# Group norm folded into per-image weights, context and attention products on quarter-width column tiles

## Chip, cores and metric

One Trainium2 chip, one of its cores. The metric is the device time of one launch in microseconds; the median of three runs of the kernel before is 2759.55 us (2758.84 to 2760.31).

## What is computed

The input x is float32 of shape (4, 128, 112, 112). Two residual blocks follow each other, each behind a group norm (32 groups of 4 channels):

```python
x = x + _L0_conv_ref(_gn(x), ...)   # layer norm over channels, 8x8 window attention, 8 heads of 16
x = x + _L1_conv_ref(_gn(x), ...)   # linear attention, depthwise 3x3, projection, batch norms, MLP
```

The second block, with t the 12544 tokens of an image:

```python
q, k, v = relu(t @ Wq + bq) * scale, relu(t @ Wk + bk), t @ Wv + bv
ctx = einsum('bhnd,bhne->bhde', k, v)      # 16x16 for each head, summed over all tokens of the image
out = einsum('bhnd,bhde->bhne', q, ctx)    # then depthwise 3x3, Wproj, batch norm 1 with t
ff = gelu(t @ Wfc1 + bfc1) @ Wfc2 + bfc2   # 128 -> 1024 -> 128, batch norm 2
```

## The kernel before, in words

Channels lie on the 128 partitions, and one whole image of float32 lies in `ximg` (128 x 12544). The work has three stages, each of which runs over the four images.

**Stage A**, window attention: `group_loop` (each engine has its own copy, with a `step` written out by hand) runs over strips of 8 rows (14 for an image, 56 in all), and in each strip over two groups, of 4 and of 3 pairs of windows (`gg` 0 and 1). A group is computed over several steps. In the step of group G, TensorE runs in this order (lines 1348 to 1381): `score_rows` of G (line 1289, coarse scores for the maxima), `out_transpose` of G-2 (1328), half 1 of `attend` of G-1 (1320, probabilities times values), `ln_transpose` of G+2 (1244), `out_project` of G-2 (1334), half 0 of `attend`, `transpose_maxima` (1295), the query and key projections of G+1 (1255 to 1257), `score_cols` (1304, 1309), `project_v` of G+1 (1272) and `ln_back` of G+2 (1250). VectorE runs `maxima` (940), `normalise` of half 1 (953, 957), `ln_stats` (911), `mt_evac` (946), `ln_moments` (919), `normalise` of half 0, in odd groups the statistics of x1 (963), `ln_norm` (926), `v_evac` of G+1 (933) and, in images 0 to 2, statistics of the next image (963) at even groups. ScalarE evacuates and does the exponentials (663); GpSimd the low halves, casts, reciprocal roots (508) and the residual (542). The query projection waits until half 1 is normalised, since they share bank 7 (line 1371).

In `attend` each 64x64 block of probabilities is the stationary operand and goes to partitions 64*w2 of the output; so two column tiles of 64 are in use, with 128 rows.

**Stage C**, keys, values and context: strips again, 896 tokens each. VectorE applies the group norm (`norm_strip`, 1050, `tfull`), ScalarE rounds to the high half (717, `tsth`), GpSimd subtracts for the low half (573, `tstl`). TensorE has per strip seven blocks of 128 tokens in four chunks (2, 2, 2, 1), one PSUM bank per chunk: `lkv` (1408) has three fp32r products of 256 columns a block. VectorE adds the bias on the way out (1060, `kv`), ScalarE the relu (724, `krel`), and `context` (1416) adds the full 128x128 product of keys and values, of which `context_masked` (1069) later keeps the diagonal 16x16 blocks. The contexts run two chunks behind (CTX_LAG). The group norm of image 3 is finished between images 0 and 1 of this stage. SyncE reloads `ximg` with the next image as strips come free (line 451).

**Stage D**, the rest of block 2: 112 blocks of 4 rows (448 tokens), with a hand-written order of its own (`step_d` on each engine, lines 793, 1168, 1491). `norm_block` (1108, `tf`), `tb_high` (740), `tb_low` (1113) and `lq` prepare the query five and four blocks ahead. A prologue of four blocks runs before `block_loop`.

An fp32 product runs as two instructions ("x" counts of the trace are instructions), an fp32r product as one. The high and low halves in fp32r make up three products in place of one in fp32.

Of the kernel before, what the change touches and what calls it, by code (L numbers as in the profile page):

```python
# [23 lines left out]
F32 = mybir.dt.float32  # L24
# [6 lines left out]
P = 128  # L31
# [26 lines left out]
CTX_LAG = 2  # L58
QW = W + 2
# [13 lines left out]
def build(nc, x_d, vec_d, fc1b_d, dw_d, wm_d, cm_d, w1_d, w2_d, sel_d, out_d):  # L73
    with ExitStack() as ctx:
# [20 lines left out]
        lws = [sb(f"lw_{n}", [P, 4, P], F32R) for n in ("hi", "lo")]  # L95
# [32 lines left out]
        stack_s = ExitStack()  # L128
        w1f = sb("w1f", [P, CM], F32, stack_s)
        sel_f = sb("sel_f", [P, 4 * P], F32, stack_s)  # L130
        stack_s.close()

        tfull = sb("tfull", [P, 2, STRIP])
        tsth = sb("tsth", [P, 2, STRIP], F32R)
        tstl = sb("tstl", [P, 2, STRIP], F32R)
        kv = sb("kv", [P, 4, 2, 2, P])
        krel = sb("krel", [P, 4, 2, P])


# [22 lines left out]
        ob = sb("ob", [P, 2, 512], F32, stack_b)  # L162
        stack_b.close()

        oring = sb("oring", [P, RING, QW])
        tf = sb("tf", [P, 2, BLOCK])
# [83 lines left out]
        tfull_ready = sem("tfull_ready")  # L250
        tsth_ready = sem("tsth_ready")
        tstl_ready = sem("tstl_ready")
        tf_ready = sem("tf_ready")
# [129 lines left out]
        def _(sp):  # L383
# [65 lines left out]
            def freed_c(i, h):  # L449
                for sp_ in range(2):  # L450
                    sp.wait_ge(tfull_ready, h * 2 + (i * STRIPS + sp_ + 1))
                    hold(sp)
                    load_next(i, h, sp_, i * (STRIPS // 2))
# [23 lines left out]
        def _(pool):  # L477
# [91 lines left out]
            def low_strips(h0, h1):  # L569
                with pool.Fori(h0, h1) as h:  # L570
                    for sp in range(2):
                        pool.wait_ge(tsth_ready, h * 2 + (sp + 1))
                        g.tensor_tensor(tstl[:, sp, :], tfull[:, sp, :], tsth[:, sp, :].bitcast(F32),
                                        ALU.subtract).then_inc(tstl_ready, 1)
            low_strips(0, STRIPS // 2 + 1)
            gn_coef(NIMG + 1, ((1, NIMG - 1),))
            low_strips(STRIPS // 2 + 1, NIMG * STRIPS // 2)
# [30 lines left out]
        def _(act):  # L608
# [3 lines left out]
            a.activation(lws[0][:], wm[:, WMATS.index("lwq"):WMATS.index("lwq") + 4, :], ACT.Copy)\  # L612
                .then_inc(weights_hi, 1)
# [101 lines left out]
            def high_strip(S, sp):  # L715
                act.wait_ge(tfull_ready, S + 1)
                a.activation(tsth[:, sp, :], tfull[:, sp, :], ACT.Copy).then_inc(tsth_ready, 1)

            def strip_c(S):
                for cc, (_, n) in enumerate(KV_CHUNKS):  # L720
                    K = S * len(KV_CHUNKS) + cc

                    act.wait_ge(kv_ready, K + 1)
                    a.activation(krel[:, cc, 0:n, :], kv[:, cc, 0:n, 0, :], ACT.Relu)\
                        .then_inc(krel_ready, 1)

            high_strip(0, 0)
            with act.Fori(0, NIMG * STRIPS // 2 - 1) as h:
                high_strip(h * 2 + 1, 1)
                strip_c(h * 2)  # L730
                high_strip(h * 2 + 2, 0)
                strip_c(h * 2 + 1)
            high_strip(NIMG * STRIPS - 1, 1)
            strip_c(NIMG * STRIPS - 2)
            strip_c(NIMG * STRIPS - 1)


            def tb_high(B, bb):
                act.wait_ge(tf_ready, B + 1)
                a.activation(tbh[:, bb, :], tf[:, bb, :], ACT.Copy).then_inc(tbh_ready, 1)  # L740

            def q_high(B, bb, prev=True, n=4):


                act.wait_ge(lq_mm, B + 1)
                if prev:
                    act.wait_ge(ql_ready, B)
                a.activation(qf[:], bank[n][:, 0:BLOCK], ACT.Relu, bias=v("blq"))
                a.activation(qh[:, bb, :], bank[n][:, 0:BLOCK], ACT.Relu, bias=v("blq"))\
                    .then_inc(qh_ready, 1)  # L750
# [42 lines left out]
            def step_d(Q, B, u, near, at):  # L793
# [3 lines left out]
                for j in range(NF):  # L797
                    hidden(B, j)
                    if j == 1 and near(4):
                        q_high(B + 4, u % 2)  # L800
                    if j == 2 and near(5):
                        tb_high(B + 5, (u + 1) % 2)
# [9 lines left out]
            tb_high(0, 0)  # L812
            tb_high(1, 1)
            q_high(0, 0, prev=False, n=0)
            tb_high(2, 0)
            q_high(1, 1, n=1)
            for k in range(2, 4):
                o_read(k - 2, k - 2, prev=False, n=4 + k)
                tb_high(k + 1, (k + 1) % 2)
                q_high(k, k % 2, n=k)  # L820
# [9 lines left out]
        def _(dve):  # L830
# [10 lines left out]
            for s in range(2):  # L841
                c = (HD + 1) * s + HD
                for b in range(2):
# [20 lines left out]
            d.tensor_tensor(lws[1][:], wm[:, WMATS.index("lwq"):WMATS.index("lwq") + 4, :],  # L864
                            lws[0][:].bitcast(F32), ALU.subtract).then_inc(weights_lo, 1)
# [92 lines left out]

            def bn_halves(dst, src):
# [29 lines left out]
            def step(G, i, s, gg, near):  # L989
# [31 lines left out]
                if gg == 1 and i == 0 and isinstance(s, int) and s == STRIPS - 1:  # L1021
                    late_low()

# [16 lines left out]
            def norm_strip(i, h, sp):  # L1040

                s = h * 2 + sp
                if i == 0:
                    dve.wait_ge(xb_loaded, ((NIMG - 1) * STRIPS + s + 1) * 16)
                else:
                    dve.wait_ge(xl_loaded[sp], ((i - 1) * (STRIPS // 2) + h + 1) * 16)
                hold(dve)
                if not (i == 0 and isinstance(h, int) and h == 0):
                    dve.wait_ge(tstl_ready, i * STRIPS + s - 1)
# [540 lines left out]
```

## Time and profile before

| | before |
|---|---|
| median of 3 runs | 2759.55 us |
| the profiled execution | 2760.2 us, span 2758.4 us |
| TensorE matmul busy | 2589.6 us (94%) |
| weight loads busy | 2131.3 us (77%) |
| VectorE | 2266.0 us (82%) |
| ScalarE | 2134.6 us (77%) |
| GpSimd | 1368.3 us (50%) |
| mean granted TensorE clock | 0.985 |

The span runs from the first instruction to the last; 1.8 us of the execution lie around it. Matmuls are pipelined, so a busy TensorE is not one at its peak; how fast it really goes is read from the distance between starts. The stages lie at 35 to 1137 us (A), 1140 to 1382 us (C) and 1411 us to the end (D).

### The profile page before, as it was taken

To read this page: it belongs to the slowest core of one execution; us is meant where nothing else is said; L and a number is where in the kernel's file an instruction comes from. 1 tells how busy PE (TensorE), PEld (TensorE's weight loads), DVE (VectorE), ACT (ScalarE), POOL (GpSimd) and SP (SyncE) were. 2 spreads that over 40 slices of the span, in tenths; PEclk is the share of its full clock that TensorE was granted. 3 is DMA by queue.
4 is the path that set the end of the run, shared out by engine and by line. 5 is a ranking of instruction groups with operands and counts; after the bars stand their busy time and mean duration, and the time that the engine had idled before them with its cause. 6 is when DMAs were issued, how large, how long until landed. Compare 5 with 4: busy or idle time off the path is not lost.

```text
span 2758.4 us, 89023 instructions
## 1 busy us (share of the span) xinstructions
PE 2589.6 (94%) x34410; PEld 2131.3 (77%) x34410; DVE 2266.0 (82%) x5003; ACT 2134.6 (77%) x3921; POOL 1368.3 (50%) x1322
## 2 busy tenths in 40 slices
PE   2999899989999999899979999999999999999999
PEld 2777677767777777799958888888888888888887
DVE  5888788888887888577788888888888888888885
ACT  2777677767777777455569999999999999999997
POOL 1555455545555555345524555555555555555454
PEclk9999999999999999899989999999999999999999
DMA  4222122222221111233301101111111011100000
GB/s 138 75 69 72 55 88 80 67 64 81 72 73 43 53 53 41 88 100 114 113 14 41 40 30 41 41 41 37 40 41 38 34 40 40 41 24 20 20 20 21
DMA packets 55773, 151.83 MB, mean 55 GB/s; under 512 B 6609, under 2 KB 20945, under 8 KB 55633
## 3 DMA queue, kind: packets, MB, share of 16 engines
q1 hardware_dynamic: 55632, 149.93, 16.9%
q8 instruction: 92, 1.51, 0.2%
q14 instruction: 49, 0.39, 0.0%
HBM read 98.52 MB, written 51.38 MB: 54 GB/s over the span
## 4 chain that ended last, share of the span: by engine, by line
PE 85%; DVE 6%; ACT 5%; issue 3%; DMA 1%; POOL 1%; DVEq 0%; SPq 0%; POOLq 0%; ACTq 0%
PE bank L1255 14%; PE bank L1257 14%; PE bank L1256 14%; PE bank L1487 12%; PE bank L1320 7%; PE bank L1309 5%; PE bank L1408 5%; ACT prob L663 4%; PE bank L1416 3%; PE bank L1334 3%; DVE vx L933 3%; PE bank L1272 2%; PE bank L1244 2%; PE bank L1304 1%; DMA ximg<-x_in 1%
## 5 line engine op out<-in xcount | busy, mean ns | idle before, releaser
L598 POOL TENSOR_TENSOR hl<-hf,hh 128x448 fp32r<-128x448 f32 x448 | 517.7, 1156 | 637.8 <-ACT hh L791 637.8
L1139 DVE SCALAR_TENSOR_TENSOR bank<-oring,dw,bank 128x448 f32<-128x448 f32 x896 | 614.9, 686 | 20.1
L1487 PE MATMUL bank<-hw,w 128*128 128x448 f32 x896 | 391.2, 538 | 0.0
L1255 PE MATMUL bank<-t1h,w_hi 128*128 128x448 f32 x896 | 365.0, 407 | 6.0 <-DVE t1l L1156 6.0
L788 ACT ACTIVATE hf<-bank,fc1b 128x448 f32<-128x448 f32 x448 | 282.6, 631 | 111.7 <-PE bank L1257 111.7
L1257 PE MATMUL bank<-t1l,w_hi 128*128 128x448 f32 x896 | 325.7, 364 | 0.0
L1256 PE MATMUL bank<-t1h,w_lo 128*128 128x448 f32 x896 | 323.1, 361 | 0.0
L1320 PEld LDWEIGHTS bank<-vx,prob 128*64 128x64 f32 x6272 | 202.9, 139 | 100.9 <-issue 83.3
L791 ACT ACTIVATE hh<-hf 128x448 fp32r<-128x448 f32 x448 | 259.2, 579 | 14.2
L782 ACT ACTIVATE hw<-bank,fc1b 128x448 f32<-128x448 f32 x448 | 265.9, 618 | 0.4 <-PE bank L1257 0.4
L940 DVE TENSOR_REDUCE mx<-bank 128x8 bf16<-128x512 f32 x448 | 248.4, 617 | 10.2 <-PE bank L1289 7.4
L514 POOL TENSOR_TENSOR xn_lo<-xn,xn_hi 128x512 fp32r<-128x512 f32 x112 | 127.1, 1135 | 249.5 <-ACT xn_hi L640 249.5
L663 ACT ACTIVATE prob<-bank 128x512 f32<-128x512 f32 x448 | 207.4, 549 | 47.2 <-PE bank L1309 46.5
L542 POOL TENSOR_TENSOR ximg<-ximg,ob 128x512 f32 (+1 forms) x112 | 127.5, 1138 | 212.2 <-ACT ob L676 212.2
L1320 PE MATMUL bank<-vx,prob 128*64 128x34 f32 x6272 | 228.3, 226 | 4.5 <-ACT prob L663 0.7
L933 DVE COPY vx<-bank 64x256 f32<-64x256 f32 x448 | 174.0, 388 | 60.7 <-PE bank L1272 55.5
L1487 PEld LDWEIGHTS bank<-hw,w 128*128 128x128 f32 x896 | 168.9, 189 | 49.4 <-issue 41.8
L1255 PE MATMUL bank<-hh,w_hi 128*128 128x448 f32 x448 | 202.0, 451 | 0.7 <-POOL hl L598 0.7
L676 ACT ACTIVATE ob<-bank,vec 128x512 f32<-128x512 f32 x112 | 71.2, 635 | 163.4 <-PE bank L1334 163.4
L1255 PEld LDWEIGHTS bank<-t1h,w_hi 128*128 128x128 f32 x896 | 168.8, 188 | 35.6 <-issue 20.8
L584 POOL TENSOR_TENSOR xw<-wb,ximg 128x448 f32<-128x448 f32 x112 | 172.6, 1541 | 45.9 <-ACT wb L773 33.4
L1256 PEld LDWEIGHTS bank<-t1h,w_lo 128*128 128x128 f32 x896 | 168.6, 188 | 31.7 <-issue 20.8
(156 smaller groups left out, 6810.8 us busy)
## 6 DMA issues: line engine op xcount, KB each, us to landing
ximg<-x SPq DMA_DIRECT2D x112, 448.0 KB, 3.4
ximg<-x_in SPq DMA_DIRECT2D x56, 448.0 KB, 3.4
x<-ximg SPq DMA_DIRECT2D x56, 448.0 KB, 2.5
y_out<-yb SPq DMA_DIRECT2D x112, 224.0 KB, 1.9
xs<-x_in SPq DMA_DIRECT2D x42, 448.0 KB, 3.4
wm<-wm_in SPq DMA_DIRECT2D x1, 512.0 KB, 4.1
w1f<-w_in SPq DMA_DIRECT2D x1, 512.0 KB, 5.3
w<-w_in SPq DMA_DIRECT2D x1, 512.0 KB, 7.4
```

What stands on the lines that cost most here:

```text
L598: g.tensor_tensor(hl[:, k, :], hf[:, k % 2, :], hh[:, k, :].bitcast(F32), ALU.subtract).then_inc(hl_ready, 1)
L663: m = a.activation(prob[:, j, 0:n // 64].rearrange("p w q -> p (w q)"), bank[j][:, 0:n], ACT.Exp)
L782: a.activation(hw[:, WHOLE_J.index(j), :], bank[j % FC1_BANKS][:, 0:BLOCK], ACT.Gelu, bias=fc1b[:, j:j + 1]).then_inc(hf_ready, 1)
L788: a.activation(hf[:, k % 2, :], bank[j % FC1_BANKS][:, 0:BLOCK], ACT.Gelu, bias=fc1b[:, j:j + 1]).then_inc(hf_ready, 1)
L791: a.activation(hh[:, k, :], hf[:, k % 2, :], ACT.Copy).then_inc(hh_ready, 1)
L933: m = d.tensor_copy(dst, src)
L1139: m = d.scalar_tensor_tensor(acc, src, dw[:, k:k + 1], acc, ALU.mult, ALU.add)
L1255: mm(out, w[0], x[0], start=start, stop=False)
L1256: mm(out, w[1], x[0], start=False, stop=False)
L1257: return mm(out, w[0], x[1], start=False, stop=stop)
L1320: m = mm(bank[6 + h][64 * w2:64 * w2 + 64, c:c + VCOLS], prob[:, j, 2 * t + w2, :], vx[:, gg, 2 * t + w2, j, :], start=True, stop=True)
L1487: m = mm(out, w2[:, j, :], hw[:, WHOLE_J.index(j), :], start=first, stop=last)
```

## The change

The group norm of block 2 is x * g + o with g and o per channel and image. It is no longer applied to the tokens. `fold_norm` scales the three weight matrices by g for each image (high and low halves in `lws`), `norm_bias` multiplies o by the weights on TensorE, and `fold_bias` adds the result to the biases (`kvb`, `qb`). ScalarE and GpSimd then make the high and low halves from `ximg` itself, in two parts of 512 and 384 columns. The relu is done in place in `kv`, which has two buffers. The context is made once a strip, one chunk pair behind, in four products of 32x32 on four column tiles in place of one of 128x128. The probabilities in `attend` are cut into quarters of 32 columns for four column tiles in place of halves of 64.

```diff
 def attend (TensorE, stage A)
-                        for w2 in range(2):
-                            c = (t % 2) * QUADS * VCOLS + j * VCOLS
-                            m = mm(bank[6 + h][64 * w2:64 * w2 + 64, c:c + VCOLS],
-                                   prob[:, j, 2 * t + w2, :], vx[:, gg, 2 * t + w2, j, :], start=True, stop=True)
+                        for q in range(4):
+                            c, w = (t % 2) * QUADS * VCOLS + j * VCOLS, 2 * t + q // 2
+                            m = mm(bank[6 + h][32 * q:32 * q + 32, c:c + VCOLS],
+                                   prob[:, j, w, 32 * (q % 2):32 * (q % 2) + 32], vx[:, gg, w, j, :],
+                                   start=True, stop=True)
 context (TensorE, stage C)
-            def context(i, K, cc, first=False, last=False):
-                n = KV_CHUNKS[cc][1]
-                pe.wait_ge(krel_ready, K + 1)
-                for t in range(n):
-                    m = mm(bank[6 + i % 2][:, 0:P], krel[:, cc, t, :], kv[:, cc, t, 1, :], ...)
+            def contexts(i, S, sp, first=False, last=False):
+                pe.wait_ge(krel_ready, S * NK + NK)
+                for cc, (_, n) in enumerate(KV_CHUNKS):
+                    for t in range(n):
+                        for j in range(QUADS):
+                            c = slice(QUAD * j, QUAD * j + QUAD)
+                            m = mm(bank[6 + i % 2][c, 0:QUAD], kv[:, sp, cc, t, 0, c], kv[:, sp, cc, t, 1, c], ...)
+                m.then_inc(ctx_mm, 1)
+            # strip_c: lkv of chunks 0 and 1, contexts of the strip before, lkv of chunks 2 and 3
 folding (VectorE; three images at the end of a strip of stage A, image 3 after image 1 of stage C)
+            def fold_norm(i):
+                d.tensor_scalar(wsc[:], wm[:, q:q + 3, :], gc[:, 1, i, 0:1], None, ALU.mult)
+                d.tensor_copy(lws[0][:, i], wsc[:])
+                d.tensor_tensor(lws[1][:, i], wsc[:], lws[0][:, i].bitcast(F32), ALU.subtract)
+                d.tensor_scalar(obc[:, i, :], cmat("ident"), 0.0, gc[:, 1, i, 1:2], ALU.mult, ALU.add)
+            def fold_bias(i, b):
+                dve.wait_ge(bias_mm, i + 1)
+                d.tensor_tensor(kvb[:, i, :], bank[b][:, 0:2 * P], cm[:, k:k + 2, :]..., ALU.add)
+                d.tensor_tensor(qb[:, i:i + 1], bank[b][:, 2 * P:2 * P + 1], v("blq"), ALU.add)
 norm_bias (TensorE)
+                pe.wait_ge(fold_ready, i * 3 + 3)
+                mm(bank[b][:, 0:2 * P], obc[:, i, :], wm[:, k:k + 2, :]...)      # 256 columns, fp32
+                mm(bank[b][:, 2 * P:2 * P + 1], wmat("lwq"), gc[:, 1, i, 1:2])   # 1 column
 stage C, ScalarE: relu in place, and the high part of two strips on after chunks 1 and 3
-                    a.activation(krel[:, cc, 0:n, :], kv[:, cc, 0:n, 0, :], ACT.Relu)
+                    a.activation(kv[:, sp, cc, 0:n, 0, :], kv[:, sp, cc, 0:n, 0, :], ACT.Relu)
+                    if ahead and cc % 2 == 1:
+                        high_part(*ahead, sp, cc // 2)
 stage C, VectorE
-            def norm_strip(i, h, sp): ... d.tensor_scalar(tfull[:, sp, :], ximg[...], gc..., gc..., ALU.mult, ALU.add)
 stage C, GpSimd: 896 columns in one piece -> 512 and 384
-                        g.tensor_tensor(tstl[:, sp, :], tfull[:, sp, :], tsth[:, sp, :], ALU.subtract)
+                        g.tensor_tensor(tstl[:, sp, c0:c0 + n], ximg[...], tsth[:, sp, c0:c0 + n], ALU.subtract)
 stage C, SyncE: the reload of a strip waits for tstl_ready in place of tfull_ready
 stage D, VectorE: norm_block (504 ns a block in the profile) goes; tb_low and ScalarE's tb_high read ximg
```

## Rows read from the trace of the kernel before

**Rows 1.** Windows by stage: us, busy us and instructions by engine, clock, DMA

```profile
35.00:1137.00 1102.00, 998.66 (x26507) 779.21 (x26507) 923.86 (x2862) 773.74 (x1348) 551.82 (x685) 0.98 0.20 65
1137.00:1210.00 73.00, 63.82 (x498) 61.64 (x499) 48.58 (x78) 36.06 (x73) 37.19 (x20) 0.90 0.37 114
1210.00:1423.00 213.00, 195.28 (x1544) 188.75 (x1543) 165.06 (x270) 123.48 (x253) 91.50 (x46) 0.94 0.30 87
1423.00:2758.00 1335.00, 1331.29 (x5863) 1101.16 (x5861) 1110.65 (x1745) 1199.07 (x2245) 684.34 (x562) 1.00 0.10 34
```

**Rows 2.** Chain of waits that ended last, 940 to 960 us: start, us, what

```profile
950.91 1.06 PE bank L1320 x32
```

**Rows 3.** Timeline of stage A, image 3, odd group: start, us, engine, instruction [idle before]

```profile
950.49 0.42 DVE L957 TENSOR_TENSOR oh<-bank,rden 128x256 f32<-128x256 f32 x1
...
951.94 0.48 PE L1255 MATMUL bank<-xn_hi,pw_hi 128*128 128x512 f32 x1
```

**Rows 4.** Timeline of stage A, image 2, odd group

```profile
700.35 1.15 DVE L963 BATCH_NORM_STATS2 gst<-xs 128x448 f32 x2
...
703.68 0.42 DVE L957 TENSOR_TENSOR oh<-bank,rden 128x256 f32<-128x256 f32 x1
...
704.26 0.48 PE L1255 MATMUL bank<-xn_hi,pw_hi 128*128 128x512 f32 x1
```

**Rows 5.** Timeline of stage A, even group: the turn of VectorE

```profile
945.15 1.37 DVE L926 TENSOR_SCALAR xc<-bank,lnmv,lnrs 128x128 f32<-128x128 f32 x4 [0.97 <-POOL lnrs L508]
...
946.53 1.46 DVE L933 COPY vx<-bank 64x192 f32<-64x192 f32 x4
```

**Rows 6.** Groups by line and shape: count | busy us, mean ns | idle before

```profile
L1320 PEld LDWEIGHTS bank<-vx,prob 128*64 128x64 f32 x6272 | 202.9, 139 | 100.9 <-issue 83.3 <-DVE vx L933 16.4 <-ACT prob L663 1.1
L1416 PEld LDWEIGHTS bank<-kv,krel 128*128 128x128 f32 x784 | 107.4, 192 | 0.7 <-ACT krel L724 0.6
L1118 DVE TENSOR_TENSOR ql<-qf,qh 128x448 fp32r<-128x448 f32 x112 | 69.2, 618 | 3.3 <-ACT qh L749 3.1
L1108 DVE TENSOR_SCALAR tf<-ximg,gc 128x448 f32 x64 | 32.2, 504 | 0.0
L1071 DVE CAST ctx_hi<-ctxm 128x128 fp32r<-128x128 f32 x4 | 0.9, 227 | 0.1
```

**Rows 7.** Timeline of weight loads: attend at 2.4 and 1.2 GHz, scores at both

```profile
700.98 1.01 PEld L1320 LDWEIGHTS bank<-vx,prob 128*64 128x64 f32 x32 [0.17 <-issue]
...
1132.66 1.79 PEld L1320 LDWEIGHTS bank<-vx,prob 128*64 128x64 f32 x32 [1.50 <-issue]
...
696.36 1.45 PEld L1309 LDWEIGHTS bank<-qs,kx 32*64 32x64 f32 x128
...
63.66 2.07 PEld L1309 LDWEIGHTS bank<-qs,kx 32*64 32x64 f32 x128 [0.20 <-issue]
```

**Rows 8.** Timeline of stage C: weight loads of one strip, and the next strip's mark

```profile
1223.48 0.53 PEld L1416 LDWEIGHTS bank<-kv,krel 128*128 128x128 f32 x4
...
1224.40 0.19 PEld L1408 LDWEIGHTS bank<-lw_lo,tsth 128*128 128x128 f32 x1
...
1224.52 0.19 PEld L1408 LDWEIGHTS bank<-lw_hi,tstl 128*128 128x128 f32 x1
...
1224.63 0.30 PEld L1416 LDWEIGHTS bank<-kv,krel 128*128 128x128 f32 x2
...
1228.68 0.31 PEld L1416 LDWEIGHTS bank<-kv,krel 128*128 128x128 f32 x2
```

**Rows 9.** Windows around the norm of image 3, columns as in rows 1

```profile
1202.00:1210.00 8.00, 4.07 (x23) 3.71 (x23) 4.90 (x9) 1.91 (x4) 3.94 (x4) 0.80 0.29 94
1210.00:1218.00 8.00, 8.00 (x58) 8.00 (x56) 4.56 (x8) 3.23 (x7) 1.32 (x1) 0.77 0.11 25
```

**Rows 10.** Timeline: start of stage C, and the prologue of stage D

```profile
1144.26 0.58 PE L1408 MATMUL bank<-lw_hi,tstl 128*128 128x256 f32 x1 [3.25 <-POOL tstl L573]
...
1398.96 0.51 DVE L1108 TENSOR_SCALAR tf<-ximg,gc 128x448 f32<-128x448 f32 x1
```

More of the change, by code:

```diff
@@ L742, in q_high, with pair @@
-            def q_high(B, bb, prev=True, n=4):
+                    if ahead and cc % 2 == 1:
+                        high_part(*ahead, sp, cc // 2)
+            for sp in range(2):
+                for k in range(NP):
+                    high_part(0, 0, sp, k)
+            for i in range(NIMG):
+                def pair(h):
+                    ahead = (i, h + 1)
+                    if isinstance(h, int) and h == STRIPS // 2 - 1:
+                        ahead = (i + 1, 0) if i + 1 < NIMG else None
+                    for sp in range(2):
+                        strip_c(i * STRIPS + h * 2 + sp, sp, ahead)
+                pair(0)
+                with act.Fori(1, STRIPS // 2 - 1) as h:
+                    pair(h)
+                pair(STRIPS // 2 - 1)
@@ L1022, in step @@
                     late_low()
+                if gg == 1 and i > 0 and isinstance(s, int) and s == STRIPS - 1:
+                    dve.wait_ge(gcoef_ready, i + 2)
+                    fold_norm(i - 1)
             def epilogue():
@@ L1037, in _, with strip_c @@
             group_loop(dve, step, prologue, epilogue)
[L1040 to L1049, printed above, removed]
[L1050 to L1053 removed]
+            def strip_c(i, S, sp):
                 for cc, (_, n) in enumerate(KV_CHUNKS):
@@ L1422, in strip_c, with norm_bias @@
                 start = isinstance(s, int) and s == 0
[L1423 removed]
                 for cc in range(NK):
[L1425 to L1434 removed]
+                    if cc % 2 == 0:
+                        pe.wait_ge(tsth_ready, S * NP + cc // 2 + 1)
+                    if not (start and i == 0):
+                        pe.wait_ge(kv_ready, S * NK + cc - NK + 1)
+                    lkv(i, S, sp, cc)
+                    if cc == CTX_LAG - 1:
+                        if not start:
+                            if isinstance(s, int) and s == 1 and i > 1:
+                                pe.wait_ge(ctxm_ready, i * 3 - 3)
+                            contexts(i, S - 1, 1 - sp, first=(isinstance(s, int) and s == 1))
+                        elif i > 0:
+                            contexts(i - 1, S - 1, 1 - sp, last=True)
+            def norm_bias(i, b):
+                pe.wait_ge(fold_ready, i * 3 + 3)
+                k = WMATS.index("lwk")
+                mm(bank[b][:, 0:2 * P], obc[:, i, :], wm[:, k:k + 2, :].rearrange("p a b -> p (a b)"),
+                   start=True, stop=True)
+                mm(bank[b][:, 2 * P:2 * P + 1], wmat("lwq"), gc[:, 1, i, 1:2], start=True, stop=True)\
+                    .then_inc(bias_mm, 1)
             pe.wait_ge(ob_ready, NG)
+            for i in range(NIMG - 1):
+                norm_bias(i, BIAS_BANKS[i])
             for i in range(NIMG):
@@ L1446, in _, with lq @@
                     pe.wait_ge(gvar_ready, NIMG + 2)
-            for cc in range(NK - CTX_LAG, NK):
-                context(NIMG - 1, NIMG * STRIPS * NK - NK + cc, cc, last=(cc == NK - 1))
-            def lq(B, bb, n=4):
+                if i == 1:
+                    norm_bias(NIMG - 1, BIAS_BANKS[NIMG - 1])
+            contexts(NIMG - 1, NIMG * STRIPS - 1, 1, last=True)
+            def lq(B, image, bb, n=4):
                 pe.wait_ge(tbh_ready, B + 1)
                 pe.wait_ge(tbl_ready, B + 1)
-                split_mm(bank[n][:, 0:BLOCK], [w[:, 0, :] for w in lws],
+                split_mm(bank[n][:, 0:BLOCK], [w[:, image, 0, :] for w in lws],
                          [tbh[:, bb, :], tbl[:, bb, :]]).then_inc(lq_mm, 1)
```

230 lines of the change are left out of this document (115 added, 115 removed).

## The prediction, made before the changed kernel ran

> **What bounds the kernel now.** I read the windows by stage first, then the groups by line and shape, then the timeline of one strip of stage A and one of stage C, because busy shares alone mislead here. Stage D is half of the time, and TensorE is busy for 1331 of its 1335 us at full clock [rows 1]. The change takes nothing from TensorE there; it takes 0.50 us a block from VectorE [rows 6], which is busy 1111 of 1335 us and waited for by nobody in steady state. So stage D should stay as it is. Whatever is won must come from stages A and C.
>
> Stage C is bound by TensorE. A strip takes 1228.68 - 1224.63 = 4.05 us [rows 8]. One `lkv` product comes every 0.12 us and one context instruction every (0.53 - 0.19) / 3 = 0.113 us [rows 8]. With 21 and 14 of them a strip that is 21 x 0.117 + 14 x 0.112 = 4.03 us: all of the period. (0.117 is what reproduces the period; the two printed starts only say 0.12.)
>
> Stage A has no single bound. In odd groups the query projection starts at 951.94, while VectorE was done with the half that it waits for at 950.49 + 0.42 = 950.91 [rows 3]: TensorE is late by 1.0 us. In images 0 to 2 VectorE has the next image's statistics, 1.15 us, in that place; it ends at 703.68 + 0.42 = 704.10 and TensorE starts at 704.26 [rows 4]: late by only 0.16. In even groups it is VectorE's own turn: xc ends at 945.15 + 1.37 = 946.52 and the evacuation of values starts at 946.53 [rows 5]. xc waited 0.97 us for GpSimd's roots, which hang on VectorE's earlier work. So a faster TensorE gives nothing in even groups.
>
> **Price of a quarter tile.** This is the term that decides. A load of 128 columns takes 192 ns and one of 64 takes 139 [rows 6]: 0.83 ns a column. `attend` issues its loads in twos, and (1.01 - 0.14) / 15 = 0.058 us lie between twos at 2.4 GHz; at 1.2 GHz, where a load lasts some 0.22, it is (1.79 - 0.22) / 15 = 0.105 us [rows 7]. 64 columns at 0.83 ns are 0.053 us (0.107 at half the clock). So the pace is that of the weight load, and both column tiles load in the same time. Moving 34 columns twice takes 28 ns at 0.83 ns each, and is hidden. The scores, on 32x64 tiles, come every (1.45 - 0.13) / 127 = 10.4 ns at full clock and (2.07 - 0.20) / 127 = 14.7 at half [rows 7]. Four tiles at a time could not beat 107 / 4 = 27 ns at half clock, since 64 columns move there; so eight tiles work at once, across column tiles too. With 32 columns the load shrinks to 27 ns and the moving stays at 28: some 33 ns for four instructions, 8.3 ns each. The scores never do better than 10.4 ns over a long batch, so I take 10.4. Bounds: 8.3 below; above, 33 ns each if four column tiles on the same 128 rows do not work at once, which no row of this kernel shows (it has two).
>
> The Trainium skill (TensorE: Matmul & The Clock Gate, The mechanism) says that a weight load overlaps running matmuls only where the row group differs. These tiles all share their rows. By it a pair in `attend` would take 53 + 28 = 81 ns, and the trace shows 58, so the row is against it; a group of four would take 27 + 28 + 5 = 60 ns, and it is the third rival below.
>
> **Stage A.** A half of two pairs goes from 32 instructions to 64: from 32 x 0.029 = 0.93 us to 64 x 0.0104 = 0.67. Of its 1.06 us on the chain [rows 2] the rest, 0.13 us, is the change of tile shape and stays. An odd group has two such halves: -0.52 us. In image 3 all of it counts (1.0 is there): 14 x 0.52 = 7.3 us. In images 0 to 2 only up to VectorE's end, 0.16 less a semaphore's 0.05, 0.11 us: 42 x 0.11 = 4.6 us. Even groups: 0. Added: `fold_norm` at the end of images 1, 2 and 3, on VectorE: 384 columns scaled (0.44, from 504 ns for 448), copied (0.4; between 0.23 for 128 columns and 0.5), subtracted (0.56, from 618 for 448), 128 columns of offset (0.25) [rows 6]: 1.65 us. The last falls into the wait for the last probabilities; two are exposed, +3.3 us. Stage A: -8.6 us.
>
> **Stage C, steady.** Contexts per strip: 7 blocks x 4 tiles x 2 = 56 instructions in place of 14: 56 x 0.0104 = 0.58 us, plus a change of tile shape in and out, two times the 0.13 above, 0.27. That makes 0.85 in place of 1.57. With 2.46 of `lkv`, 3.31 us. The contexts of a strip wait for its last relu. That chain is: the last product's end, 0.2 us of latency, the last evacuations on VectorE (up to 1.0 us behind), ScalarE's 0.3. It ends about 1.35 to 1.45 us into the next strip, where TensorE gets there at 1.40; I add 0.04. New period 3.35 us, 0.70 less; 55 strips and the first: -39 us. Bounds: 0.47 us for the batch and no wait, 3.2 us (-47); or 0.4 us of wait, 3.7 (-19). The other engines fit under 3.35: VectorE 4.0 - 0.75 of its work goes, 2.5; ScalarE 1.54 for relus and 1.1 for two parts, 2.65; GpSimd 1.27 + 1.0, 2.3 (estimates from the same shapes elsewhere in stage A and C). The reload of `ximg` starts after GpSimd in place of after VectorE, some 3 us later, for an image that is needed a whole image later: nothing, and if that cover went, the transfer of each strip would stand before its high half. DMA share is 0.30 to 0.37 [rows 1].
>
> **Stage C, ends.** At the start TensorE waits 3.25 us for the first low half [rows 10]. The new first part is 512 columns and saves 0.8; the three `norm_bias` (about 3.6 us at the low clock) lie under that wait. -1. Between images 1 and 2 a new stop: VectorE has the last evacuations (1.0), the context of image 0 (0.86), `fold_norm` (1.65); then `norm_bias` (0.6) on TensorE. That is 4.1 us, and the stop after image 0, which left TensorE busy for 4.1 of 8 us, was followed by a granted clock of 0.77 over the next 8 us [rows 9], the lower level of 1.2 GHz for a part of it, which is 8 x 0.23 = 1.8 us of full speed lost. I take half of that for the shorter stop (bounds 0 and 1.8): +5 us. Stage D's prologue loses `norm_block` and the round trip behind it, once fully on the path (0.51 [rows 10] and 0.64 for ScalarE's answer), the others in part: -2.5.
>
> **Sum**: -8.6 - 39 - 1 + 5 - 2.5 = -46 us. Against the profiled execution's 2760.2 us that is 2714; the median lies 0.65 us below that execution, which changes nothing: 2714 us.
>
> **Rivals.**
> 1. The contexts wait for the relu (chance 0.14). ScalarE has a part of 0.6 us between the relus of chunks 1 and 2. If that pushes the last relu back by 0.4 us, every strip of stage C pays it: 56 x 0.4 = 22 us, 2736. For it: the margin is under 0.1 us. Against: VectorE sends chunk 2 later than that part ends.
> 2. Column tiles take turns (0.11), the slower end. Place: `attend` and contexts. Price: 33 ns for each instruction. A half of two pairs then takes 2.1 us in place of 0.93; 3.5 of them a strip are +4.1 us, less 0.3 of slack, x 56 = +213; contexts are 1.87 + 0.27 against 1.57, +0.57 x 56 = +32; with the +5 and the small terms about 3010 us. It decides from the pace at which 64 instructions outlast 0.93 us, 14.6 ns each, plus the slack of 0.08 a half: above some 16 ns it is slower. Against it: the twos in attend and eights in the scores.
> 3. Loads are not hidden behind the other tiles (0.08): 15 ns each. `attend` 0.96 against 0.93, no gain in A (+3.3 from folding, +2 in odd groups); contexts 0.84 + 0.27 = 1.11, -0.46 x 56 = -26; with the ends 2741.
> 4. Only two column tiles at a time (0.05), 33 ns for two: 16.7 ns each. `attend` +0.14 a half, less slack, +10; contexts 0.94 + 0.27, -20; the ends +4: 2755, no change by measurement.
>
> **The numbers.** The forecast has 0.62, with 2692 to 2733 by its own bounds (C 8 lower or A twice as much; a longer stop or a relu wait above). The range 2690 to 2750 takes in rivals 1 and 3 and leaves out 2, 4 and the ends of the forecast, 0.2 in all. Within 0.2% (5.5 us, about what a measurement tells from no change) lies rival 4: 0.05. Slower: rival 2, 0.11. Faster: 0.84.
>
> **What the profile would show.** Right: stage C some 38 us shorter with a strip every 3.3 to 3.4 us; line 1320's successor with 12544 instructions at 8 to 11 ns; stage A's strips 0.1 us shorter in images 0 to 2 and 0.5 in image 3; stage D within 2 us of 1335. Wrong: instructions of `attend` more than 16 ns apart, TensorE waiting for the relu by more than 0.2 us a strip, or a clock of 1.2 GHz between images that outlasts 10 us.

## The result, and the profile after

The change makes the kernel a little faster: 2738.49 us, median of 4 runs (2737.89 to 2739.3), against 2759.93 for the kernel before (4 runs beside it, 2758.84 to 2760.38). The ratio is 0.992, with a 95% interval of 0.9904 to 0.9936. The forecast was 2714 us. Of the 46 us that it expected, 21 came.

The windows of the kernel after by stage, with columns as in [rows 1], and behind them stage D of a kernel told of below (e5), the same but for a larger `qb` that moves the tiles behind it by 224 bytes:

```profile
35.00:1137.00 1102.00, 948.00 (x32786) 716.11 (x32787) 927.20 (x2874) 776.42 (x1353) 554.99 (x687) 0.98 0.20 65
1137.00:1341.00 204.00, 195.20 (x4328) 183.90 (x4326) 143.63 (x254) 133.49 (x334) 130.50 (x115) 0.96 0.45 131
1341.00:1380.00 39.00, 25.42 (x82) 20.17 (x83) 29.51 (x48) 24.96 (x45) 6.88 (x6) 0.69 0.00 1
1380.00:2736.00 1356.00, 1352.49 (x5855) 1099.05 (x5854) 1068.38 (x1636) 1197.69 (x2243) 684.53 (x562) 1.00 0.10 34
```

```profile
1380.00:2714.00 1334.00, 1330.21 (x5859) 1100.95 (x5857) 1080.61 (x1637) 1197.12 (x2244) 684.55 (x562) 1.00 0.10 34
```

Stage C takes some 37 us less, as forecast. Stage D, with the same products, the same clock (1.00) and TensorE busy from end to end, takes 1356 us where e5 takes 1334 for the same work. The results of stage D, `yb`, show it best: one for each of 112 blocks, so first to last start is the stage. The kernel before, and then the kernel after (engine, operation, count, duration, first and last start; then what VectorE waited for):

```profile
L1165 DVE SCALAR_TENSOR_TENSOR yb<-bank,par,xw x112: 682/684/686, 1425.2 to 2755.1; 128x448 f32<-128x448 f32 x112
...
  PE bank L1487: 130.5, 112
```

```profile
L1198 DVE SCALAR_TENSOR_TENSOR yb<-bank,par,xw x112: 682/684/685, 1379.9 to 2733.1; 128x448 f32<-128x448 f32 x112
...
  PE bank L1535: 152.4, 112
```

The first result comes 45.3 us earlier, close to the 46.1 us that the forecast had for everything ahead of it. The last comes only 22.0 us earlier. Stage D went from 1329.9 to 1353.2 us, 12.01 to 12.23 us a block, and VectorE waits for TensorE 22 us more. So the expected gain was there and was given back in a stage whose instructions on TensorE are the same.

Where in a block? The timeline of TensorE in stage D, kernel after (start, duration, instruction):

```profile
2003.59 0.37 PE L1284 MATMUL bank<-t1l,w_hi 128*128 128x448 f32 x1
2003.79 0.36 PE L1282 MATMUL bank<-t1h,w_hi 128*128 128x448 f32 x1
2003.99 0.37 PE L1283 MATMUL bank<-t1h,w_lo 128*128 128x448 f32 x1
2004.20 0.37 PE L1284 MATMUL bank<-t1l,w_hi 128*128 128x448 f32 x1
2004.41 0.37 PE L1282 MATMUL bank<-tbh,lw_hi 128*128 128x448 f32 x1
2004.61 0.37 PE L1283 MATMUL bank<-tbh,lw_lo 128*128 128x448 f32 x1
...
2011.73 0.37 PE L1284 MATMUL bank<-hl,w_hi 128*128 128x448 f32 x1
2011.93 0.36 PE L1282 MATMUL bank<-qh,ctx_hi 128*128 128x448 f32 x1
2012.13 0.36 PE L1283 MATMUL bank<-qh,ctx_lo 128*128 128x448 f32 x1
```

The five steps from 2003.59 to 2004.61 are 204 ns each on average. No row has an idle time before it. Means over 1500 to 2700 us, from the starts of the trace: `t1h,w_lo` to `t1l,w_hi` takes 205.8 ns after and 197.5 before, `t1h,w_hi` to `t1h,w_lo` 205.7 and 200.8, while the fp32 products (`hw,w`) take 375 in both. A block has 45 such products; 45 x some 5 ns x 112 = 25 us. One family is an exception: `qh,ctx_hi` to `qh,ctx_lo` takes 0.20 (198 ns by the unrounded starts).

Two explanations fit so far. One (X): VectorE and ScalarE now read `ximg` in stage D and the norm's pass is gone, so the engines get in each other's way more than before. The other (P): placement. The change adds buffers, among them `qb` with 16 bytes a partition, and tiles are laid one behind the other in steps of 32 bytes. From the list of allocations of the two kernels, start addresses in a partition modulo 256:

```
            w1, w2s, lw, pj   ctx   stage D's moving tiles   xn_hi  pw   tsth
before             64          64            128               160   64    96
after              64          96            160               192   96   192
```

The moving tiles of stage D stand 64 bytes above their weights before, and 96 above them after; `qh` alone still stands 64 above its `ctx`, and it is the fast one.

### The profile page after: what moved, and what is told of

Its sections match the earlier page's. It is cut to its first block, busy times and chain, and to the rows that moved or that the text cites. A ratio compares the mean times of both kernels' runs of the same rounds, so it can differ in the third digit from the quotient of the medians.

```text
span 2736.4 us, 106560 instructions
## 1 busy us (share of the span) xinstructions
PE 2521.7 (92%) x43050; PEld 2019.7 (74%) x43050; DVE 2186.2 (80%) x4859; ACT 2134.5 (78%) x3977; POOL 1380.4 (50%) x1378
## 4 chain that ended last, share of the span: by engine, by line
PE 72%; DVE 18%; issue 4%; ACT 2%; POOL 2%; DMA 1%; DVEq 0%; SPq 0%; POOLq 0%; ACTq 0%
PE bank L1282 14%; PE bank L1283 14%; PE bank L1284 14%; PE bank L1535 12%; DVE mx L967 7%; PE bank L1437 6%; PE bank L1336 4%; DVE vx L960 3%; PE bank L1299 2%; ACT prob L672 2%; DVE gst L1012 1%; PE bank L1347 1%; DVE xc L953 1%; PE bank L1450 1%; POOL lnrs L514 1%
## 5 line engine op out<-in xcount | busy, mean ns | idle before, releaser
L1283 PE MATMUL bank<-t1h,w_lo 128*128 128x448 f32 x896 | 330.3, 369 | 0.0
L1347 PEld LDWEIGHTS bank<-vx,prob 128*32 128x32 f32 x12544 | 131.7, 110 | 109.1 <-issue 90.1
L1198 DVE SCALAR_TENSOR_TENSOR yb<-bank,par,xw 128x448 f32<-128x448 f32 x112 | 76.5, 683 | 152.4 <-PE bank L1535 152.4
L953 DVE TENSOR_SCALAR xc<-bank,lnmv,lnrs 128x128 f32<-128x128 f32 x392 | 134.4, 402 | 58.4 <-POOL lnrs L514 58.3
```

What stands on the lines that cost most here:

```text
L1283: mm(out, w[1], x[0], start=False, stop=False)
```

## The experiments

The groups of runs were taken on different chips. The kernel before has medians of 2760.6, 2763.4, 2761.7 and 2760.7 us in them, and its single runs go from 2752 to 2770, 0.3% to either side. So where a few us matter I read the stage from the trace. Stage D repeats to 0.1 us in the nine kernels whose distances there are 64 bytes; stages A and C do not, as is told below.

**e1: move everything behind `qb` by 32 bytes.**

```diff
-        qb = sb("qb", [P, NIMG])
+        qb = sb("qb", [P, 16])
```

> The kernel after, with qb (16 bytes a partition) given 64 bytes, so that ctx, the stage-A tiles and all tiles of stage D move up by 32 bytes and stage D's moving tiles start at a multiple of 64 bytes again, as its weights do and as both did before. Nothing is computed otherwise. Theory P (placement: an fp32r product runs some 5 ns longer when its weights and its moving tile stand 32 bytes apart modulo 64): the distance between products of 448 columns in stage D goes back from 203-208 ns to 197-202, the block from 12.23 to 12.01 us, stage D is 23 us shorter: 2715 us (2711 to 2720). Theory X (VectorE and ScalarE now read ximg for the high and low halves, and the norm's pass is gone, so the engines collide otherwise in SBUF): no effect of the shift, 2738, block 12.23.

Measured: 2734.89 us, median of 5 (2731.02 to 2737.48), ratio 0.9909 (0.9892 to 0.9925). Stage D 1345.8 us, 12.16 a block. Products take 196 to 211 ns in a pattern of five steps, some 203.5 on average. A miss for both: the shift made stage D 7 us shorter, which X doesn't foresee, but it did not repair it.

**e2 and e3: the kernel before, shifted.** e2 moves only the tiles of stage D by 32 bytes, and the weights stay; e3 moves weights and tiles alike.

```diff
 e2
+        pad_d = sb("pad_d", [P, 8])
         oring = sb("oring", [P, RING, QW])
 e3
+        pad_w = sb("pad_w", [P, 8])
         w1s = [sb(f"w1_{n}", [P, CM], F32R) for n in ("hi", "lo")]
```

> The kernel before, with 32 unused bytes ahead of oring, so that only the tiles of stage D move, to 32 modulo 64; weights and ctx stay at 0. Theory P: all 45 fp32r products of a block (ctx's three too, which stay fast in the kernel after) take 5 ns more, 45 x 5 x 112 = 25 us: 2783 to 2788, block 12.23 to 12.25. Theory X: 2760, block 12.01.

> The kernel before, with 32 unused bytes ahead of w1, so that the weights and everything behind them move alike: weights and moving tiles of stage D both at 32 modulo 64, the stage-A tiles at 0. Theory P, relative (what counts is that both have the same offset): 2760, block 12.01. Theory P, absolute (what counts is the moving tile's own start): 2783 to 2788, block 12.23. Theory X: 2760.

Measured: e2 2785.53 us (4 runs, 2781.48 to 2788.67), ratio 1.0093 (1.0074 to 1.0113); e3 2756.85 (10 runs), ratio 0.999 (0.9979 to 1.0001). In e2, 32 unused bytes cost 25 us in a kernel that has none of the change. Its results and its products:

```profile
L1166 DVE SCALAR_TENSOR_TENSOR yb<-bank,par,xw x112: 682/684/685, 1425.6 to 2780.2; 128x448 f32<-128x448 f32 x112
...
  PE bank L1488: 154.1, 112
```

```profile
2000.99 0.37 PE L1258 MATMUL bank<-t1l,w_hi 128*128 128x448 f32 x1
2001.20 0.36 PE L1256 MATMUL bank<-t1h,w_hi 128*128 128x448 f32 x1
2001.40 0.37 PE L1257 MATMUL bank<-t1h,w_lo 128*128 128x448 f32 x1
2001.61 0.37 PE L1258 MATMUL bank<-t1l,w_hi 128*128 128x448 f32 x1
```

Stage D is 1354.6 us, 12.24 a block, and the products are some 205 ns apart, like those of the kernel after. In e3 stage D is 1329.9 us again. So the absolute address doesn't count: what counts is the distance between weights and moving tile, and a change of it alone costs as much as the kernel after lost. Both are in the kernel before, so X could still have a share in the kernel after; e5 decides that. That distance modulo 256 was 64 in the fast kernels (before, e3, and `qh` on `ctx` after), 96 in the slow ones (after, e2) and 128 in e1. My first wording, "the same offset modulo 64", was wrong, which is why the forecast for e1 missed.

**e5: 64 bytes apart.** `qb` gets 256 bytes, so that all distances of stage D are 64 again.

```diff
-        qb = sb("qb", [P, NIMG])
+        qb = sb("qb", [P, 64])
```

> The kernel after with qb given 256 bytes: stage D's moving tiles now start 64 bytes above their weights modulo 256 (128 against 64), as in the kernel before, and qh 64 above ctx. Theory Q, formed after the first four runs: not 'same offset modulo 64' but 'moving tile and weights 64 bytes apart' (modulo 128 or 256) makes a product of 448 columns take 200 ns; 32 apart it takes 205.5, 0 or 128 apart 204. All four runs and the fast product qh-ctx of the kernel after fit it. So here: 200.0 ns a product, block 12.01 us, stage D (first to last result) 1330 us, 2715 us (2708 to 2720). Theory X (other readers of ximg, no placement effect in this kernel): 2735 to 2738, block 12.2.

Measured: 2711.66 us, median of 5 (2710.58 to 2716.17), ratio 0.9813 (0.9796 to 0.983). Results and products of e5:

```profile
L1198 DVE SCALAR_TENSOR_TENSOR yb<-bank,par,xw x112: 682/684/685, 1381.1 to 2711.0; 128x448 f32<-128x448 f32 x112
...
  PE bank L1535: 130.6, 112
```

```profile
2005.77 0.36 PE L1283 MATMUL bank<-t1h,w_lo 128*128 128x448 f32 x1
2005.97 0.37 PE L1284 MATMUL bank<-t1l,w_hi 128*128 128x448 f32 x1
2006.17 0.36 PE L1282 MATMUL bank<-t1h,w_hi 128*128 128x448 f32 x1
2006.37 0.36 PE L1283 MATMUL bank<-t1h,w_lo 128*128 128x448 f32 x1
2006.57 0.36 PE L1284 MATMUL bank<-t1l,w_hi 128*128 128x448 f32 x1
```

200 ns a step, stage D 1329.9 us, VectorE's wait back at 130.6 (130.5 before). The forecast for e5 was 2715 us and 12.01 us a block. Nothing else of the change was touched, and nothing of the 23 us is left for X. This settles the cause of the miss, and it is a version that beats both kernels.

**e6: the other fp32r products too.** Unused bytes ahead of `xn_hi` and `tsth` put `pw` and `lw` 64 bytes from them as well.

```diff
+        pad_x = sb("pad_x", [P, 56], F32, stack_b)
         xns = [sb(f"xn_{n}", [P, 2, 512], F32R, stack_b) for n in ("hi", "lo")]
+        pad_t = sb("pad_t", [P, 32], F32, stack_b)
         tsth = sb("tsth", [P, 2, STRIP], F32R, stack_b)
```

> As the run before, and also xn_hi and xn_lo 64 bytes above pw (they were 96 above in both kernels) and lw's key and value part 64 above tsth (it was 224 above in the kernel before, 128 in the one after). By theory Q lkv's 21 products a strip go from 119.5 to some 117 ns, 56 x 21 x 2.5 ns = 3 us; the query and key projections (6 products a group) become some 5 ns shorter each, 0.03 us a group, at most 3 us over 112 groups, of which half may lie beside other work: 4 us below the run before, 2711 (2706 to 2715). Rival: these products are bound by their weight loads (a product of 256 columns, loads of 128), so nothing changes against the run before.

Measured: 2711.9 us, median of 5, the same as e5, so the 4 us that the forecast had do not come. `lkv` had little left to win: the steps between its products are 118.5 to 118.8 ns in the kernel after (1250 to 1340 us, distance 128), but 117.5 to 117.9 already in e5 (160) and 117.4 here (64); they are 119.4 to 120.3 in e1 (96). The projections of 512 columns do get shorter, `xn_hi,pw_lo` to `xn_lo,pw_hi` from 235.6 to 230.4 ns (100 to 1100 us), those of 384 columns by less, 175.4 to 173.8. But the same step of 512 columns takes 231.7 in the kernel before, at the old distance of 96, so something else moves it as well. And an ordinary strip of stage A goes only from 18.51 to 18.49 us. So distances other than 64 are not slow for every fp32r product.

**e7 and e8: a sweep of distances.** Stage D's tile families were each given another distance.

```diff
 e7: pads of 192, 224, 160, 96 and 192 bytes ahead of tbh, qh, dwh, t1h and hh
 e8: pads of 128, 224, 96, 160 and 64 bytes ahead of the same
+        pad_tbh = sb("pad_tbh", [P, 48])
         tbh = sb("tbh", [P, 2, BLOCK], F32R)
```

> The kernel after with its stage-D tiles set apart by unused bytes, so that each pair has another distance from weights to moving tile modulo 256: tb 32, q 224, dw 160, t1 0, hh 192. Start to start of the products inside each family tells the price of each distance. If only the distance modulo 128 counts: hh (192) 200 ns, t1 (0) 204 as at 128, the odd ones (32, 224, 160) 205.5. If it is modulo 256: hh too is slow, 204 to 206. Time as a whole: between 2728 and 2740.

> The same with the distances turned: tb 224, q 160, dw 32, t1 192, hh 0. Modulo 128: t1 at 200 ns (24 of the 45 products), hh 204, the rest 205.5, and the whole 2723 to 2730. Modulo 256: t1 204 to 206 and 2735 to 2742.

One run each, so only the traces count: 2730.82 and 2731.26 us, stage D 1343.0 and 1342.3. Mean ns from the first product of a family to the second, and from the second to the third:

```
distance   family and kernel                     1st->2nd          2nd->3rd
  0        t1 in e7; hh in e8                    203.2; 203.1      203.1; 207.1
 32        tb in e7; dw in e8                    200.8; -          201.7; 205.0
 64        t1, hh, tb, q in e5; q in e1          200.8 to 200.9; 201.3   197.5 to 197.6; 199.1
 96        t1 in after; hh in after              205.7; 203.4      205.8; 206.6
128        t1 in e1; hh in e1                    203.5; 206.7      203.6; 203.3
160        q in e8; dw in e7                     202.5; -          205.0; 204.2
192        t1 in e8; hh in e7                    202.6; 203.1      200.5; 201.0
224        q in e7; tb in e8                     203.3; 203.3      206.6; 205.8
```

(dw's first step has an fp32 product before it that overlaps it, and is left out.) Neither expectation holds as written. 192 is not as good as 64, so modulo 128 is not the rule; it is not as bad as the rest either, and e8's 2731 lies between the two forecasts. Each family's steps also hang on the families beside it, whose distances differ here, so this is a rough map. What stands: 64 gave 199 to 200 ns on average inside a family, the others 201 to 206, with 32 and 192 the nearest to 64 and 96 the slowest of all.

**e4: `attend` in quarters in the kernel before.**

```diff
-                        for w2 in range(2):
-                            c = (t % 2) * QUADS * VCOLS + j * VCOLS
-                            m = mm(bank[6 + h][64 * w2:64 * w2 + 64, c:c + VCOLS],
-                                   prob[:, j, 2 * t + w2, :], vx[:, gg, 2 * t + w2, j, :], start=True, stop=True)
+                        for q in range(4):
+                            c, w = (t % 2) * QUADS * VCOLS + j * VCOLS, 2 * t + q // 2
+                            m = mm(bank[6 + h][32 * q:32 * q + 32, c:c + VCOLS],
+                                   prob[:, j, w, 32 * (q % 2):32 * (q % 2) + 32], vx[:, gg, w, j, :],
+                                   start=True, stop=True)
```

> The kernel before with attend alone in quarters (64 instructions of 32 columns for a half of two pairs in place of 32 of 64). As forecast: a half takes 0.80 in place of 1.06 us on the chain, image 3 is 7 us shorter, images 0 to 2 4.6 us, 2748 us. Rival (quarters cost as much as they save or VectorE sets the end in all images): -0 to -3 us, 2757 to 2760. Stage A of the kernel after was 4.3 us shorter with fold_norm's +3.3 in it, so -7.6 to -8 is what these two terms leave to it: 2752.

Measured: 2753.38 us, median of 10, ratio 0.9974 (0.9964 to 0.9984), near the 2752 that the kernel after had left and not the forecast's 2748. The trace, by the evacuations of `ob` (28 to an image), gives image 1, 2 and 3 as 268.6, 267.5 and 253.8 us, against 267.4, 267.4 and 262.2 before: -8.4 in image 3, nothing won in images 1 and 2. Windows over single strips, from one evacuation to that of the next strip: image 1 strips 10 and 11 and image 3 strip 10, kernel before, then e4:

```profile
529.09:547.69 18.60, 17.40 (x477) 13.59 (x477) 16.56 (x52) 13.77 (x24) 9.78 (x12) 1.00 0.24 77
547.69:570.53 22.84, 18.97 (x481) 14.94 (x481) 18.38 (x59) 13.83 (x24) 11.33 (x16) 0.93 0.16 58
...
1062.59:1081.19 18.60, 17.40 (x477) 13.59 (x477) 15.45 (x50) 13.78 (x24) 9.77 (x12) 1.00 0.15 49
```

```profile
530.74:549.24 18.50, 16.60 (x596) 12.54 (x598) 16.48 (x52) 13.75 (x24) 9.76 (x12) 1.00 0.24 76
549.24:572.95 23.71, 19.29 (x600) 15.11 (x602) 18.25 (x58) 13.82 (x24) 11.33 (x16) 0.86 0.17 58
...
1057.40:1075.20 17.80, 16.33 (x596) 12.42 (x599) 15.43 (x50) 13.76 (x24) 9.77 (x12) 1.00 0.15 52
```

An ordinary strip of image 1 is 0.10 us shorter, as forecast (0.11); the strip with the norm's statistics is 0.87 longer, at a granted clock of 0.86 in place of 0.93. Much is given back in the first strips of images 1 and 2, which take 22.65 and 21.89 us in place of 19.92 and 19.76, the one at a granted clock of 0.85 in place of 1.00, the other at 1.00 in both. So the clock is not all of it, and why these strips get longer is open. Image 3's strips are 0.80 us shorter, more than the 0.52 forecast.

**e9 and e10: undo one half of the quarters in e5.**

```diff
 e9, contexts (and the whole mask in context_masked)
-                        for j in range(QUADS):
-                            c = slice(QUAD * j, QUAD * j + QUAD)
-                            m = mm(bank[6 + i % 2][c, 0:QUAD], kv[:, sp, cc, t, 0, c], kv[:, sp, cc, t, 1, c],
+                        m = mm(bank[6 + i % 2][:, 0:P], kv[:, sp, cc, t, 0, :], kv[:, sp, cc, t, 1, :],
 e10: attend's four quarters back to two halves (the diff of e4, reversed)
```

> e5 (the kernel after, operands 64 bytes apart) with the contexts as one whole product of 128 x 128 columns for each token block again, still one batch per strip and still without the norm's pass. As forecast the quarters are what makes the strip shorter: 14 instructions at 0.112 in place of 56 at 0.0104 and two changes of shape, 1.57 against 0.85 us, so a strip of stage C takes 4.03 us, the stage 40 us more, 2752 us. Rival (part of the gain comes from the norm's pass that left VectorE, or from waits that went with it, and would stay without the quarters): a strip of 3.6 to 3.8 us, 2728 to 2740.

> e5 with attend in halves of 64 columns again (the other half of the change's quarters undone). From the run with quarters added to the kernel before: images 0 to 2 unchanged (268, 271, 271 us an image), image 3 8 to 10 us longer (252 to 261), so +8 to +10: 2720 us. Forecast's own terms: +12, 4.6 of it in images 0 to 2: 2724.

e9: 2756.02 us, median of 10, ratio 0.9983 (0.9969 to 0.9997). From the last `ob` to the first `yb` it takes 283.7 us, e5 243.4: +40.3, the forecast's 40. Weight loads of two strips of e9:

```profile
1226.90 0.64 PEld L1446 LDWEIGHTS bank<-kv 128*128 128x128 f32 x5
1227.46 0.19 PEld L1435 LDWEIGHTS bank<-lw_hi,tsth 128*128 128x128 f32 x1
...
1229.95 1.64 PEld L1446 LDWEIGHTS bank<-kv 128*128 128x128 f32 x14
1231.51 0.19 PEld L1435 LDWEIGHTS bank<-lw_hi,tsth 128*128 128x128 f32 x1
```

1231.51 - 1227.46 = 4.05 us a strip, the period of the kernel before [rows 8]. (The medians of e9 and e5 are 44 us apart, on two chips.) The quarters alone make stage C's gain, and the norm's pass that left VectorE gives nothing by itself. Whether the quarters could be had without folding the norm was not tried.

e10: 2725.88 us, median of 4, ratio 0.9877 (0.9852 to 0.9902). Its images 1 and 2 take 270.8 and 271.3 us (e5: 271.7 and 271.2), image 3 262.2 (e5: 251.5): +10.7 there, nothing elsewhere, as e4 said from the other side. The median is 14 us above e5's and above both forecasts (2720 and 2724), the profiled span 7 us (2721.3 against 2714.4); the two ran on different chips, and I go by the images.

**e11 and e12: where `fold_norm` costs.** In the kernel after the last strips of images 1 and 2 are longer.

```diff
 e11 (on e6)
-                if gg == 1 and i > 0 and isinstance(s, int) and s == STRIPS - 1:
+                if gg == 0 and i > 0 and isinstance(s, int) and s == STRIPS - 1:
 e12 (on e6)
+                if i == NIMG - 1 and isinstance(s, int) and s == 0:
+                    dve.wait_ge(gcoef_ready, i + 1)
+                    fold_norm(gg)
-                if gg == 1 and i > 0 and isinstance(s, int) and s == STRIPS - 1:
+                if gg == 1 and i == NIMG - 1 and isinstance(s, int) and s == STRIPS - 1:
```

> e6 (all operands 64 bytes apart) with fold_norm of stage A issued in the even group of an image's last strip, where VectorE has the next image's statistics (1.15 us) in other strips and nothing in this one, in place of the odd group. Theory F: fold_norm's 1.7 us are exposed in images 1 and 2 because VectorE sets the pace there, and now only what is over 1.15 is: some 2 us an image less, image 1 and 2 at 268 in place of 270 to 271, 2708 us. Rival (what lengthens images 1 and 2 is not fold_norm, or its place does not matter): 2711 to 2712, images 1 and 2 at 270 to 271.

> e6 with the folds of images 0 and 1 moved out of images 1 and 2 into the first two groups of image 3, where every odd group has slack on VectorE (the strip there is 17.8 and not 18.5 us, set by TensorE). The last strip of images 1 and 2 takes 20.83 and 22.18 us in e6. Theory F (fold_norm is what lengthens them): 18.4 and 20 as in the kernel before with quarters alone, image 3 at most 2.5 us longer, 2709 (2706 to 2711). Rival G (these strips move with the granted clock after the stop for the statistics, 0.85 to 0.93 there, whoever does what in them): they stay between 20 and 23 in sum as before, 2711 to 2714.

e11: 2712.23 us, median of 5, images 1 and 2 at 272.4 and 269.3 us (e6: 270.1 and 269.3), where theory F had 268. The place inside the strip gains nothing. e12: 2714.78 us, median of 5, against 2709 by theory F. The last strips of images 1 and 2 fall from 20.83 and 22.18 us to 18.41 and 19.94, as theory F said: `fold_norm` is what lengthens them, by 2.4 and 2.2. But the first strip of image 3, which now has both folds, takes 24.66 us in place of 18.29, 6.4 more, where at most 2.5 were forecast. So there is no slack for it there, and moving it loses. In busy time `fold_norm` takes 2.4 us on VectorE and not the 1.65 of the forecast. That is its first instruction, here in the last strip of image 2 of the kernel after (groups of VectorE, 866 to 886 us):

```profile
L991 DVE TENSOR_SCALAR wsc<-wm,gc 128x384 f32<-128x384 f32 x1 | 1.2, 1216 | 0.0
...
L995 DVE TENSOR_TENSOR lw_lo<-wsc,lw_hi 128x384 fp32r<-128x384 f32 x1 | 0.6, 559 | 0.0
L993 DVE CAST lw_hi<-wsc 128x384 fp32r<-128x384 f32 x1 | 0.4, 359 | 0.0
L996 DVE TENSOR_SCALAR obc<-cm,gc 128x128 f32<-128x128 f32 x1 | 0.3, 280 | 0.0
```

1216 ns for a multiplication that takes 0.42 us in stage C (below). The trace shows what it met: GpSimd's subtraction `xn_lo` had begun 0.01 us before it (868.10, 1.01 us), and it ended 0.21 us after that one's end. So it is with the same instruction in image 1 (597.35), and with the copy of 1.03 us in stage C beside GpSimd's `tstl`; where no instruction of GpSimd was running when they began, the two take 0.40 to 0.42 and 0.36 us in every trace here. In e11 none was, `fold_norm` is back at 1.6 us, and images 1 and 2 are still no shorter. So this meeting explains the busy time and not what a fold costs the strip.

## Why the prediction was wrong, and where it was right

**The step that failed** is "The change takes nothing from TensorE there ... So stage D should stay as it is", with its mark "stage D within 2 us of 1335". It counted instructions, and they are the same. It took for granted that an fp32r product costs the same wherever its operands lie, though the change's new buffers move every tile behind them. The price of such a product belonged in the sum as a term of its own: 23.3 us. The check is e5, the same change with the old distances: 2711.66 us, against 2714 (by the profiled spans 44.0 us below the kernel before, by the medians beside it 51.8). None of the four rivals named this; rival 1 and rival 3 had about the right total (2736 and 2741) for reasons that the trace refutes. That 2738 lies inside 2690 to 2750 is luck too, since the range was drawn that wide for those two rivals.

**Stage C: right.** Two strips of the kernel after, the weight loads of the contexts:

```profile
1219.18 0.58 PEld L1450 LDWEIGHTS bank<-kv 128*32 128x32 f32 x56
...
1222.50 0.21 PEld L1450 LDWEIGHTS bank<-kv 128*32 128x32 f32 x14
```

3.32 us a strip (3.31 in most), forecast 3.35. Last `ob` to last context is 205.5 us after and 243.0 before, -37.4; forecast -39 -1 +5 = -35. The stop after image 0, which the forecast left as it was, adds 5.2 us to two strips in place of 7.7, and that makes up for the longer one below. Rival 1's wait for the relu did not appear: the contexts' loads (L1450, in the groups below) waited for ScalarE's `kv` for 1.5 us in the whole kernel.

**The price of a quarter: slightly better than forecast.** Start to start at full clock, `attend` and the contexts both take 9.1 ns an instruction (medians of the batches; 9.2 and 9.4 as means over all, slower clock included). That lies between the lower bound, 8.3, and the 10.4 that the forecast took from the scores. The groups of the kernel after:

```profile
L1347 PEld LDWEIGHTS bank<-vx,prob 128*32 128x32 f32 x12544 | 131.7, 110 | 109.1 <-issue 90.1 <-DVE vx L960 17.7 <-ACT prob L672 1.2
...
L1450 PEld LDWEIGHTS bank<-kv 128*32 128x32 f32 x3136 | 33.4, 112 | 9.1 <-ACT kv L741 1.5 <-issue 0.5
```

A load of 32 columns lasts 110 ns in the profile, and a new one begins every 9: loads overlap deeply although these tiles share all their rows. Rivals 2, 3 and 4 asked for 33, 15 and 16.7 ns. Rival 3 was the rule of the Trainium skill (TensorE: Matmul & The Clock Gate, The mechanism) that a weight load overlaps running matmuls only where the row group differs; by it the contexts would have won 26 us, and e9 against e5 shows 40.3. The measurement is against the rule for tiles that share rows.

**Stage A: half of the forecast at best.** From the start to the last `ob` it is -4.3 us, forecast -8.6, and that pair of traces flatters it. The last `ob` starts at 1138.7, 1138.4 and 1135.5 us in the kernel before, e2 and e3, which have the same stage A, and between 1134.4 and 1139.6 in seven kernels with the change's (after, e1, e5 to e9): 0.3 us earlier by the means. Image 3 won more than the 7.3 forecast (8.4 in e4, 10.7 in e10, 9.8 by the means), since the pace is 9.1 and not 10.4. Images 0 to 2 lost all of it again, 2.6, 4.0 and 2.9 us by the means, where the forecast had 4.6 won and 3.3 lost. "42 x 0.11 = 4.6 us" failed: the 0.10 is there in each ordinary strip, but the strips around the statistics give it back (e4: +1.2 in image 1, 0 in image 2), some of them at a lower granted clock. And "1.65 us" for `fold_norm` was 2.4 in busy time; its strips got longer by 2.0 to 3.5 us (after against e4) and by 3.3 and 4.1 (e10 against the kernel before). Why image 0, which has no fold, got longer is open.

**The stop between images 1 and 2: nearly right in length, too cheap in clock.** The kernel after, timeline and windows:

```profile
1239.30 0.42 DVE L991 TENSOR_SCALAR wsc<-wm,gc 128x384 f32<-128x384 f32 x1
1239.36 1.21 POOL L580 TENSOR_TENSOR tstl<-ximg,tsth 128x384 fp32r<-128x384 f32 x1 [0.38 <-ACT tsth L734]
1239.75 1.03 DVE L993 CAST lw_hi<-wsc 128x384 fp32r<-128x384 f32 x1
1240.82 0.56 DVE L995 TENSOR_TENSOR lw_lo<-wsc,lw_hi 128x384 fp32r<-128x384 f32 x1
1241.30 0.28 DVE L996 TENSOR_SCALAR obc<-cm,gc 128x128 f32<-128x128 f32 x1
1241.63 0.50 PEld L1476 LDWEIGHTS bank<-wm,obc 128*128 128x128 f32 x2 [4.11 <-DVE obc L996]
```

```profile
1232.00:1240.00 8.00, 5.73 (x147) 5.17 (x145) 6.13 (x13) 5.38 (x14) 5.68 (x6) 1.00 0.53 157
1240.00:1248.00 8.00, 6.37 (x79) 5.90 (x80) 3.42 (x7) 1.35 (x3) 0.76 (x2) 0.57 0.24 74
```

TensorE's load waits 4.11 us, where 4.1 was forecast for the wait and `norm_bias` together. Then the granted clock is 0.57 over 8 us: 1.2 GHz for 6.83 us, from 1240.96, which is 3.4 us of full speed lost where the forecast took 0.9. Two batches of contexts there come 10.01 and 4.08 us after the ones before them, 7.5 more than two strips, about the sum of the wait and the lost speed; forecast 5, with 5.9 as the upper bound. Stage D's prologue, last context to first `yb`, is 3.6 us shorter (forecast 2.5).

The sum ahead of stage D, -46.1 forecast and -45.3 measured, is therefore right partly by luck: stage A 4 us short, stage C 2 and the prologue 1 us over. By the means over all kernels with the same work ahead of stage D it is -43.

## What to carry to other kernels

A change that adds or resizes a buffer moves every tile behind it. Where TensorE sets the pace, compare the start-to-start distance of products that the change did not touch before you trust a count of instructions, and look at the addresses if it differs. Here a distance of 64 bytes (modulo 256) between weights and moving tile, in place of 96, was worth 23 us of 2738 and cost one line; and a pad that keeps later tiles where they were is a cheap control for any edit of the layout.

## What the runs showed of the hardware

An fp32r product of 128x128 weights and 448 columns starts 200 ns after the one before when its moving tile lies 64 bytes above its weights modulo 256, and 201 to 206 on average at the other seven multiples of 32 that were tried, with no other engine's work changed (96 in the kernel after and in e2, the others in e1, e7 and e8). The Trainium skill (SBUF — State Buffer, SBUF: two separate sides) says that on the engine side only the port pair shared by VectorE and GpSimd causes contention and that TensorE never waits on anyone. For VectorE and GpSimd the traces fit that: a multiplication by a scalar of 128x384 took 1.20 to 1.22 us when GpSimd's subtraction had begun up to 0.02 us before it, and 0.40 to 0.42 without one. They also show that TensorE's own pace depends on where its two operands lie. That weight load and moving reads meet in the memory would fit, but no run shows it, and why `lkv` is all but as fast at 160 as at 64 is open. Column tiles of 32 columns on the same 128 rows run at 9.1 ns an instruction: two quarters take 18.2 ns in place of the 29.1 of one half.
